# A two-layer convolution block on one core: the first convolution of images 3 to 7 in 64x32 tiles with a half-exchanged copy, and a new order of the work around it

## The chip, the cores and the metric

The kernel runs on one core of a Trainium2 chip. Its five engines run programs of their own and meet only at semaphores: TensorE (PE), VectorE (DVE), ScalarE (ACT), GpSimd (POOL), and SyncE (SP), which issues the DMAs. The metric is the device time of one execution in microseconds (us).

## The reference

Eight images of 32 channels, 128x128 pixels, float32. Cut to what is computed:

```python
x = x + conv0(quantised(_gn(x))) * (sx * sw / 127**2) + bias   # 3x3, int8 values, one scale sx over all eight images
h = lrelu(instnorm(disco_conv(_gn(x), weight1)))               # 3x3 kernel from a fixed basis
x = x + lrelu(instnorm(disco_conv(h, weight2)))
# _gn: GroupNorm over 2 channels; instnorm: per image and channel
```

The disco kernels are zero at the four corners of their 3x3 window, so convolutions 1 and 2 have five taps, convolution 0 has nine. The scale `sx` needs the largest value over all images, so no convolution starts before all images are read and normalised once. After that each image goes through three convolutions, and each of the later two needs statistics over a whole image of what came before it.

## The kernel before

An image is stored as four quadrants of pixels (even and odd rows and columns), each with 32 channels on 32 partitions, so 128 partitions by 64x64 numbers. A tap that shifts by one pixel is then a move to another quadrant, for half of the output with a shift of one place in a tile padded to 66x66. A **unit** is 16 of an image's 64 rows, 1024 columns, in two PSUM banks; an image has four. The tile `ring` has three slots of one unit each, which the three convolutions fill in the order `ORDER` (convolution 1 of image t, convolution 0 of image t+2, convolution 2 of image t). `wait_slot` holds a unit back until the unit three places before it has been taken out of its slot.

**TensorE.** Convolution 0 (`conv0_pair`, line 1023 in the profile) reads the float16 tile `qpad` with matmuls of 128 rows by 32 columns of the array. Four of them, for the four output quadrants, run side by side: a *round*. A bank takes four rounds (own, side, vert, corn), a unit 8, an image 32. Convolutions 1 and 2 (`half_taps`, lines 965 and 971) read float32 tiles with matmuls of 64 rows by 32 columns. Eight run side by side, four writing one bank (L965), four the other (L971), and each matmul shows as two records in the trace. Such a convolution of a unit is a `first_half` and a `second_half`, with the row halves exchanged between the banks; the second half waits until the first has ended (`crossed`). `conv` orders them first 0, first 1, second 0, first 2, second 1, first 3, second 2, second 3. A `gather` (L929) is a small 128x128 matmul that adds statistics across partitions.

**VectorE** goes through `period(t)`: statistics of each unit of convolutions 1 and 2 (`conv_stats`, L810) straight from `ring`; at an image's end `spread_conv` (L817, L819), on which the gather waits, and `group_moments` (L718), which reads the gather's result; `x1_unit` (L794), which adds convolution 0's unit to x and so empties its slot; `x1_stats` (L800) on the sum; `output` (L827), the last addition of the image before.

**ScalarE** takes units of convolutions 1 and 2 out of `ring` after their statistics (`take`, L381), which empties the slot, and normalises: `make_h` (L404) makes the input of convolution 2, `make_a` (L394) that of convolution 1 of the next image, `norm_out` (L413) the part that `output` adds.

**GpSimd** turns moments into scales and shifts (`norm_c`, `norm_x1`: L539 to L551) and quantises image t+3 in `period` t in four pieces of three operations each (`quantise`: L619, L622, L627). The third writes `qpad`, the first of an image not before convolution 0 has finished the image before.

**SyncE** loads the images, and stores each finished one in two pieces (the last in four), in order.

A *period* is the stretch from one image's convolution 1 to the next one's. The one in which TensorE works on images 3 (convolutions 1 and 2) and 5 (convolution 0) stands for all below.

## Time and profile before

| | us |
|---|---|
| median of 3 runs (387.83 to 388.05) | 387.9 |
| the profiled execution: its time | 387.43 |
| the profiled execution: its span | 385.6 |
| PE busy | 298.4 |
| DVE busy | 278.2 |
| ACT busy | 234.8 |
| POOL busy | 159.9 |

The span runs from the first instruction to the last; 1.8 us of the profiled execution's time lie around it. The first 76 us read and normalise the images; from there to 370 us TensorE hardly stops. In the profile a row "x4" of PE is a group of four matmuls that start together; the distance from one row's start to that of the next round is the pace, and the duration beside it includes the way through the array.

### The profile page before, as it was taken

Reading aid. Unit: us, or ns where it says so; the run is one execution under the profiler, and the core shown is the slowest. Engines: PE = TensorE matmul, PEld = TensorE weight load, DVE = VectorE, ACT = ScalarE, POOL = GpSimd, SP = SyncE. Lnnn points to the kernel's source line nnn. Section 1 sums busy time; section 2 is a strip of 40 time slices with the busy share of each in tenths; the row PEclk is TensorE's granted clock in tenths of the full one; section 3 lists DMA queues with packets and bytes.
Section 4 is the critical chain, followed back from the end, with each engine's and each line's share of the span. In section 5 each row is a group of like instructions: output and inputs, shape, how many; then the busy total and the mean of one; then the engine's idle time right before and its main releaser. Section 6 shows DMA issues by size and latency. Waiting matters only on the chain.

```text
span 385.6 us, 11585 instructions
## 1 busy us (share of the span) xinstructions
PE 298.4 (77%) x5224; PEld 121.5 (31%) x5224; DVE 278.2 (72%) x418; ACT 234.8 (61%) x243; POOL 159.9 (41%) x248
## 2 busy tenths in 40 slices
PE   0000100297999999999999999999999999999950
PEld 0000100253343334333433343333334343333320
DVE  3828899879969559857974995599559857544575
ACT  1079996295534674476528654754674478856554
POOL 0189886338949622932492067209621002100100
PEclk9999999999999999999999999999999999999985
DMA  7999600000000005001400220050005001400055
GB/s 272 398 426 428 267 1 1 0 2 2 3 2 2 3 2 220 3 2 59 164 3 3 115 106 3 3 219 4 2 2 221 2 2 58 165 3 2 2 219 218
DMA packets 4176, 34.77 MB, mean 90 GB/s; under 512 B 608, under 2 KB 768, under 8 KB 1280
## 3 DMA queue, kind: packets, MB, share of 16 engines
q1 hardware_dynamic: 4128, 34.04, 21.6%
q8 instruction: 41, 0.67, 0.7%
q14 instruction: 7, 0.06, 0.1%
HBM read 17.26 MB, written 16.78 MB: 88 GB/s over the span
## 4 chain that ended last, share of the span: by engine, by line
PE 60%; DVE 27%; POOL 5%; issue 3%; DMA 2%; ACT 1%; SPq 0%; DVEq 0%; POOLq 0%
PE ring L965 46%; PE ring L1023 8%; DVE amax L745 8%; DVE xs L827 7%; DVE bn_c L810 6%; PE ring L971 4%; DMA xs<-w_dram 2%; POOL apad L571 2%; DVE xs L794 2%; PE gathered_in L929 1%; DVE bn_x L800 1%; DVE bn_x L723 1%; ACT scaled L364 1%; POOL xs L510 1%; DVE qpad L787 1%
## 5 line engine op out<-in xcount | busy, mean ns | idle before, releaser
L810 DVE BATCH_NORM_STATS2 bn_c<-ring 128x6 f32<-128x512 f32 x128 | 82.7, 687 | 59.3 <-PE ring L971 59.3
L539 POOL TENSOR_SCALAR var_eps_c<-moments_c 128x1 f32<-128x1 f32 x16 | 3.1, 192 | 166.2 <-DVE moments_c L718 166.2
L971 PE MATMUL ring<-apad,own 64*32 64x512 f32 x448 | 58.7, 591 | 0.0
L965 PE MATMUL ring<-apad,own 64*32 64x512 f32 x448 | 58.6, 590 | 0.0
L971 PE MATMUL ring<-hpad,own 64*32 64x512 f32 x448 | 58.6, 591 | 0.0
L965 PE MATMUL ring<-hpad,own 64*32 64x512 f32 x448 | 58.6, 590 | 0.0
L971 PE MATMUL ring<-apad,side 64*32 64x512 f32 x448 | 58.4, 588 | 0.0
L965 PE MATMUL ring<-apad,vert 64*32 64x512 f32 x448 | 58.3, 587 | 0.0
L971 PE MATMUL ring<-hpad,side 64*32 64x512 f32 x448 | 58.3, 587 | 0.0
L965 PE MATMUL ring<-hpad,vert 64*32 64x512 f32 x448 | 58.2, 587 | 0.0
L381 ACT COPY apad<-ring 128x1024 f32<-128x1024 f32 x28 | 28.4, 1013 | 47.8 <-DVE bn_c L810 47.1
L381 ACT COPY hpad<-ring 128x1024 f32<-128x1024 f32 x28 | 28.4, 1014 | 27.8 <-DVE bn_c L810 27.3
L404 ACT ACTIVATE hpad<-hpad,shift_c,scale_c 128x1024 f32<-128x1024 f32 (+2 forms) x28 | 32.8, 1235 | 14.7 <-POOL shift_c L551 14.7
L413 ACT ACTIVATE apad<-apad,shift_c,scale_c 128x1024 f32<-128x1024 f32 x28 | 34.1, 1242 | 12.0 <-POOL shift_c L551 12.0
L794 DVE SCALAR_TENSOR_TENSOR xs<-ring,dequant,xs 128x1024 f32<-128x1024 f32 x32 | 39.9, 1274 | 1.9 <-PE ring L1023 1.9
L800 DVE BATCH_NORM_STATS2 bn_x<-xs 128x6 f32<-128x512 f32 x64 | 39.4, 678 | 0.0
L394 ACT ACTIVATE apad<-xs,shift_x,scale_x 128x1024 f32<-128x1024 f32 (+2 forms) x28 | 33.2, 1238 | 4.7 <-POOL shift_x L548 4.7
L827 DVE SCALAR_TENSOR_TENSOR xs<-apad,bias,xs 128x1024 f32<-128x1024 f32 x28 | 35.0, 1269 | 0.0
L745 DVE TENSOR_REDUCE amax<-apad 128x1 f32<-128x4096 f32 (+1 forms) x7 | 26.3, 3788 | 8.4 <-POOL apad L571 8.4
L619 POOL TENSOR_SCALAR scaled<-xs,q_scale,q_shift 128x1024 f32<-128x1024 f32 (+2 forms) x24 | 28.8, 1201 | 0.0
L331 ACT ACTIVATE qpad<-xs 128x4096 f16<-128x4096 f32 x5 | 18.0, 3608 | 16.9 <-DMA xs<-x_dram 16.9
L1042 PE MATMUL gathered_gn<-spread_x,const 128*128 128x24 f32 x6 | 1.8, 388 | 32.3 <-DVE spread_x L731 32.3
(139 smaller groups left out, 622.7 us busy)
## 6 DMA issues: line engine op xcount, KB each, us to landing
xs<-x_dram SPq DMA_DIRECT2D x8, 2048.0 KB, 10.1
out_dram<-xs SPq DMA_DIRECT2D x14, 1024.0 KB, 4.3
out_dram<-xs SPq DMA_DIRECT2D x4, 512.0 KB, 2.8
xs<-w_dram SPq DMA_DIRECT2D x1, 288.0 KB, 9.2
const<-const_dram SPq DMA_DIRECT2D x1, 146.0 KB, 2.4
xs<-w_dram SPq DMA_DIRECT2D x1, 36.0 KB, 1.7
bias<-bias_dram SPq DMA_DIRECT2D x1, 0.5 KB, 2.3
```

What stands on the lines that cost most here:

```text
L381: nc.scalar.copy(unit_of(tile, u), grid(slot(v, t, u))).then_inc(taken[v], 1)
L394: nc.scalar.activation(rows_of(a_tile(b), r0, r1), grid(xs_rows(b, r0, r1)), ACT.Identity, bias=param(shift["x1"], b), scale=param(scale[" ...
L404: nc.scalar.activation(rows, rows, ACT.Prelu, bias=param(shift["c1"], t), scale=param(scale["c1"], t), alpha=SLOPE).then_inc(h_ready, 1)
L413: nc.scalar.activation(rows, rows, ACT.Prelu, bias=param(shift["c2"], t), scale=param(scale["c2"], t), alpha=SLOPE).then_inc(out_norm, 1)
L745: nc.vector.tensor_reduce(amax[:, n:n + 1], gn_tile(b)[:, c0:c1], AX.X, ALU.max, apply_absolute_value=True).then_inc(max_done, 1)
L794: nc.vector.scalar_tensor_tensor(x, slot(0, b, u), dequant[:], x, ALU.mult, ALU.add).then_inc(taken[0], 1)
L800: ins = nc.vector.bn_stats(bn["x1"][:, k, :], xs_cols(b, k * BANK, BANK))
L810: ins = nc.vector.bn_stats(bn[s][:, u * UBANKS + h, :], ring_of(v, t, u)[:, h, :])
L827: nc.vector.scalar_tensor_tensor(x, unit_of(a_tile(t), u), bias[:], x, ALU.add, ALU.add).then_inc(out_ready, 1)
L965: nc.tensor.matmul(bank_out(t, u, v, hp, C * (2 * px + py), C), wv[q0:q0 + 64, v - 1, px, py, :], window(tile, u * UBANKS + hp, dy, 0, q0, ...
L971: ins = nc.tensor.matmul(bank_out(t, u, v, hx, C * (2 * px + py), C), ws[q0:q0 + 64, v - 1, px, py, :], window(tile, u * UBANKS + hx, 0, d ...
L1023: ins = nc.tensor.matmul(bank_out(b, u, 0, h, C * (2 * px + py), C), w[:, px, py, :], window(tile, u * UBANKS + h, dy, dx), start=part == ...
```

## The change

1. **Convolution 0 of images 3 to 7** is no longer done by `conv0_pair` but by `taps0`, in 64x32 tiles: six groups of four matmuls for a half unit, eight of them side by side, so 3 rounds for a half unit, 6 for a unit and 24 for an image. The nine taps fit because a second float16 tile `qturn` holds `qpad` with its two partition halves exchanged; the corner tap reads it in one of the two banks (`turn0` are its weights), where the other bank reads the side tap from `qpad`. `first0` waits for `qturn` (semaphore `q_turned`), `second0` for the end of its `first0` (`crossed0`).
2. **`turn(b)`** on SyncE fills `qturn` with two DMAs of 64 partitions once image b is quantised and convolution 0 of image b-1 is done. It stands in SP's queue between the stores of images.
3. **Order on TensorE** (`conv0_and_2`): the gather of convolution 1's statistics stands behind three half units; `first_half(2, t, 0)` stands in front of `second0(b, 3)`.
4. **Order on VectorE** in `period`, for all images: `group_moments("c1", t)` directly behind `spread_conv(1, t)`, the four `x1_unit`s together, two of the four `output`s of the image before behind them, and `x1_stats` mixed with the statistics of convolution 2.
5. **Room**: one tile `scaled` in place of two. It also holds `kern` and `kern0`, and small tiles share one. `quantise` therefore waits for each earlier piece, ScalarE's first quantising steps write to `hpad` without a wait for VectorE, GpSimd waits once for `weights12_ready`, and ScalarE makes four more small copies for `turn0`.

The diff, cut to its core:

```diff
@@ -96,7 +96,8 @@
         qpad = sb("qpad", [P, PAD, PAD], F16)
-        scaled = [sb(f"scaled{p}", [P, QCOLS], F32) for p in range(2)]
+        qturn = sb("qturn", [P, PAD, PAD], F16)
+        scaled = sb("scaled", [P, QCOLS], F32)
...
@@ -137,12 +133,13 @@
         var_eps_x = sb("var_eps_all", [P, B], F32)
-        kern = sb("kern", [P, 2 * TAPS * C], F32)[0:C].rearrange("p (v k o) -> p v k o", v=2, k=TAPS)
-        kern0 = sb("kern0", [P, TAPS * C], F16)[0:C].rearrange("p (k o) -> p k o", o=C)
-        centre = sb("centre", [P, 1], F32)
-        var_eps = {s: sb(f"var_eps_{s}", [P, 1], F32) for s in STAGES[1:]}
-        scale = {s: sb(f"scale_{s}", [P, 2], F32) for s in STAGES[1:]}
-        shift = {s: sb(f"shift_{s}", [P, 2], F32) for s in STAGES[1:]}
+        kern = scaled[0:C, 0:2 * TAPS * C].rearrange("p (v k o) -> p v k o", v=2, k=TAPS)
+        kern0 = scaled[0:C, 2 * TAPS * C:].bitcast(F16)[:, 0:TAPS * C].rearrange("p (k o) -> p k o", o=C)
+        var_eps_tile = sb("var_eps", [P, 3], F32)
+        var_eps = {s: var_eps_tile[:, n:n + 1] for n, s in enumerate(STAGES[1:])}
+        params = sb("params", [P, 2, 6], F32)
+        scale = {s: params[:, 0, 2 * n:2 * n + 2] for n, s in enumerate(STAGES[1:])}
+        shift = {s: params[:, 1, 2 * n:2 * n + 2] for n, s in enumerate(STAGES[1:])}
...
@@ -247,6 +246,9 @@
         gn_cut = COLS // 2
+        TURNED = 3
...
@@ -291,6 +293,17 @@
                 load(b)
+            def turn(b):
+                if b > TURNED:
+                    sp.wait_ge(conv_done[0], UNITS * b)
+                sp.wait_ge(q_ready, 4 * b)
+                for half in range(2):
+                    to, at = 64 * half, 64 * (1 - half)
+                    sp.dma_start(qturn[to:to + 64, 1:1 + BLK, :], qpad[at:at + 64, 1:1 + BLK, :]).then_inc(q_turned, 16)
+            turn(TURNED)
             for t in range(B):
...
@@ -298,12 +311,14 @@
                                  xs_cols(t, n * cols, cols)).then_inc(stored_first if t < 4 else stored, 16)
+                if t + 4 < B:
+                    turn(t + 4)
             sp.wait_ge(stored_first, 16 * 8)
             sp.wait_ge(stored, 16 * (2 * (B - 5) + 4))
         @block.scalar
         def _(act):
-            def assemble(kernel, own, side, vert, corn):
+            def assemble(kernel, own, side, vert, corn, turned):
...
@@ -317,7 +332,8 @@
                         if corn is not None:
-                            last = nc.scalar.copy(corn[q, 1 - qx, 1 - qy, :], k[:, 1 - dx, 1 - dy, :])
+                            nc.scalar.copy(corn[q, 1 - qx, 1 - qy, :], k[:, 1 - dx, 1 - dy, :])
+                            last = nc.scalar.copy(turned[q, qx, 1 - qy, :], k[:, 1 + dx, 1 - dy, :])
                 return last
...
@@ -359,15 +375,14 @@
                 r0, r1 = EDGES[n:n + 2]
-                if n >= 2:
-                    act.wait_ge(q_ready, n - 1)
-                nc.scalar.activation(scaled[n % 2][:, 0:(r1 - r0) * BLK], xs_rows(0, r0, r1), ACT.Identity,
+                nc.scalar.activation(flat(hpad)[:, r0 * BLK:r1 * BLK], xs_rows(0, r0, r1), ACT.Identity,
                                      bias=q_shift[:, 0:1], scale=q_scale[:, 0:1]).then_inc(q_scaled, 1)
             def affine_one(n):
                 r0, r1 = EDGES[n:n + 2]
+                act.wait_ge(q_ready, n + 1)
                 nc.scalar.activation(flat(hpad)[:, r0 * BLK:r1 * BLK], xs_rows(1, r0, r1), ACT.Identity,
...
@@ -613,9 +628,9 @@
                 r0, r1 = EDGES[n:n + 2]
-                rows = scaled[n % 2][:, 0:(r1 - r0) * BLK]
+                rows = scaled[:, 0:(r1 - r0) * BLK]
                 at = 4 * (b - 2) + n
-                pool.wait_ge(q_ready, 4 * (b - 1) + max(n - 1, 0))
+                pool.wait_ge(q_ready, 4 * (b - 1) + n)
                 nc.gpsimd.tensor_scalar(rows, xs_rows(b, r0, r1), q_scale[:, b:b + 1], q_shift[:, b:b + 1],
...
@@ -638,6 +653,7 @@
             norm_x1(0)
+            pool.wait_ge(weights12_ready, 1)
             quant_pieces(2, 0)
...
@@ -839,26 +856,24 @@
                     output(t - 1, 1)
-                    output(t - 1, 2)
                 conv_stats(1, t, 2)
-                if before:
-                    output(t - 1, 3)
                 conv_stats(1, t, 3)
                 spread_conv(1, t)
                 if t == 0:
                     group_moments("x1", 1)
-                x1_unit(t + 2, 0)
                 group_moments("c1", t)
-                x1_unit(t + 2, 1)
+                for u in range(UNITS):
+                    x1_unit(t + 2, u)
+                if before:
+                    output(t - 1, 2)
+                    output(t - 1, 3)
                 x1_stats(t + 2, 0)
-                x1_unit(t + 2, 2)
-                x1_unit(t + 2, 3)
+                conv_stats(2, t, 0)
                 x1_stats(t + 2, 1)
                 x1_stats(t + 2, 2)
+                conv_stats(2, t, 1)
                 x1_stats(t + 2, 3)
                 spread_stats("x1", t + 2)
-                conv_stats(2, t, 0)
-                conv_stats(2, t, 1)
                 conv_stats(2, t, 2)
...
@@ -993,10 +1008,11 @@
-            def conv(v, t, gathers=()):
-                first_half(v, t, 0)
+            def conv(v, t, gathers=(), begun=False):
+                if not begun:
+                    first_half(v, t, 0)
                 first_half(v, t, 1)
...
@@ -1027,6 +1043,53 @@
+            def taps0(b, u, hp, start, stop):
+                hx = 1 - hp
+                for n in range(3):
+                    for px in range(2):
+                        for py in range(2):
+                            q0, dy = 64 * px, 1 if py else -1
+                            tile, w, dy, dx = ((qpad, own0, 0, 0), (qpad, vert0, dy, 0),
+                                               (qturn, turn0, dy, 1 if px else -1))[n]
+                            nc.tensor.matmul(bank_out(b, u, 0, hp, C * (2 * px + py), C), w[q0:q0 + 64, px, py, :],
+                                             window(tile, u * UBANKS + hp, dy, dx, q0, 64),
+                                             start=start and n == 0, stop=stop and n == 2)
+                    for px in range(2):
+                        for py in range(2):
+                            q0, dx, dy = 64 * (1 - px), 1 if px else -1, 1 if py else -1
+                            w, dy, dx = ((own0, 0, 0), (vert0, dy, 0), (side0, 0, dx))[n]
+                            ins = nc.tensor.matmul(bank_out(b, u, 0, hx, C * (2 * px + py), C), w[q0:q0 + 64, px, py, :],
+                                                   window(qpad, u * UBANKS + hx, dy, dx, q0, 64),
+                                                   start=start and n == 0, stop=stop and n == 2)
+                return ins
+            def first0(b, u):
+                wait_slot(0, b, u)
+                pe.wait_ge(q_turned, 32 * (b - TURNED + 1))
+                taps0(b, u, 0, True, False).then_inc(crossed0, 1)
+            def second0(b, u):
+                pe.wait_ge(crossed0, UNITS * (b - TURNED) + u + 1)
+                taps0(b, u, 1, False, True).then_inc(conv_done[0], 1)
+            def conv0_and_2(b, t):
+                first0(b, 0)
+                first0(b, 1)
+                second0(b, 0)
+                gather("c1", t)
+                first0(b, 2)
+                second0(b, 1)
+                second0(b, 2)
+                first0(b, 3)
+                first_half(2, t, 0)
+                second0(b, 3)
+                conv(2, t, begun=True)
             counts = [0, 0]
...
@@ -1055,11 +1118,14 @@
                 conv(1, t, [("c2", t - 1), ("x1", t + 1)] if t >= 1 else ())
-                conv0_pair(t + 2, 0, gather_after=("x1", 1) if t == 0 else None)
-                conv0_pair(t + 2, 1, gather_after=("c1", t))
-                conv0_pair(t + 2, 2)
-                conv0_pair(t + 2, 3)
-                conv(2, t)
+                if t + 2 >= TURNED:
+                    conv0_and_2(t + 2, t)
+                else:
+                    conv0_pair(t + 2, 0, gather_after=("x1", 1))
+                    conv0_pair(t + 2, 1, gather_after=("c1", t))
+                    conv0_pair(t + 2, 2)
+                    conv0_pair(t + 2, 3)
+                    conv(2, t)
             conv(1, B - 2, [("c2", B - 3), ("x1", B - 1)])
```

VectorE in a period, from the statistics of convolution 1's third unit. In the rows of before, L810 are `conv_stats`, L827 `output`, L794 `x1_unit`, L800 `x1_stats`, L718 the moments:

```order
L810 BN_STATS bn_c<-ring 128x6 x2
L827 SCALAR_TENSOR_TENSOR xs<-apad,bias,xs 128x1024
L810 BN_STATS bn_c<-ring 128x6 x2
L817 BN_AGGR own_stat_c<-bn_c 128x2
L819 TENSOR_TENSOR spread_c<-const,own_stat_c 128x12
L794 SCALAR_TENSOR_TENSOR xs<-ring,dequant,xs 128x1024
L718 BN_AGGR moments_c<-gathered_in 128x2
L794 SCALAR_TENSOR_TENSOR xs<-ring,dequant,xs 128x1024
L800 BN_STATS bn_x<-xs 128x6 x2
L794 SCALAR_TENSOR_TENSOR xs<-ring,dequant,xs 128x1024 x2
L800 BN_STATS bn_x<-xs 128x6 x6
```

The same place in the changed kernel, where L827 are `conv_stats`, L844 `output`, L811 `x1_unit`, L817 `x1_stats`, L735 the moments:

```order
L827 BN_STATS bn_c<-ring 128x6 x4
L834 BN_AGGR own_stat_c<-bn_c 128x2
L836 TENSOR_TENSOR spread_c<-const,own_stat_c 128x12
L735 BN_AGGR moments_c<-gathered_in 128x2
L811 SCALAR_TENSOR_TENSOR xs<-ring,single,xs 128x1024 x4
L844 SCALAR_TENSOR_TENSOR xs<-apad,single,xs 128x1024 x2
L817 BN_STATS bn_x<-xs 128x6 x2
L827 BN_STATS bn_c<-ring 128x6 x2
L817 BN_STATS bn_x<-xs 128x6 x4
L827 BN_STATS bn_c<-ring 128x6 x2
L817 BN_STATS bn_x<-xs 128x6 x2
```

An output stood between the statistics of the third and the fourth unit, and another in front of the third; now two stand behind the fourth `x1_unit`, ahead of the statistics of convolution 2's first unit.

TensorE at the end of convolution 0, before: its last bank, then the first half of convolution 2's first unit (L965 and L971).

```order
L1023 MATMUL ring<-qpad,own 32x512 x4
L1023 MATMUL ring<-qpad,side 32x512 x4
L1023 MATMUL ring<-qpad,vert 32x512 x4
L1023 MATMUL ring<-qpad,corn 32x512 x4
L965 MATMUL ring<-hpad,own 32x512 x4
L971 MATMUL ring<-hpad,own 32x512 x4
L965 MATMUL ring<-hpad,vert 32x512 x4
L971 MATMUL ring<-hpad,side 32x512 x4
```

The same place now: the last rows of `first0(b, 3)` (L1057 and L1064 are `taps0`), the first half of convolution 2's first unit (L980 and L986), and `second0(b, 3)`.

```order
L1057 MATMUL ring<-qturn,turn 32x512 x4
L1064 MATMUL ring<-qpad,side 32x512 x4
L980 MATMUL ring<-hpad,own 32x512 x4
L986 MATMUL ring<-hpad,own 32x512 x4
L980 MATMUL ring<-hpad,vert 32x512 x4
L986 MATMUL ring<-hpad,side 32x512 x4
L1057 MATMUL ring<-qpad,own 32x512 x4
L1064 MATMUL ring<-qpad,own 32x512 x4
L1057 MATMUL ring<-qpad,vert 32x512 x4
L1064 MATMUL ring<-qpad,vert 32x512 x4
L1057 MATMUL ring<-qturn,turn 32x512 x4
L1064 MATMUL ring<-qpad,side 32x512 x4
```

Two groups of four make a round of eight here, and convolution 0's last half unit has moved behind four rows of convolution 2.

## Rows read from the trace of the kernel before

**Rows 1.** The page: busy time, and TensorE and its granted clock in 40 slices.

```profile
PE 298.4 (77%) x5224; PEld 121.5 (31%) x5224; DVE 278.2 (72%) x418; ACT 234.8 (61%) x243; POOL 159.9 (41%) x248
...
PE   0000100297999999999999999999999999999950
...
PEclk9999999999999999999999999999999999999985
```

**Rows 2.** Busy time by stretch (from:to, length, then each engine's): five periods; convolution 0 of one.

```profile
132.77:313.63 180.86, 180.20 (x3238) 70.20 (x3230) 135.27 (x210) 109.27 (x101) 69.49 (x106) 1.00 0.15 61
...
219.74:227.58 7.84, 7.70 (x146) 3.58 (x145) 7.60 (x11) 4.26 (x4) 3.26 (x5) 1.00 0.45 181
```

**Rows 3.** TensorE's timeline, end of convolution 1 to convolution 2: start, duration, what.

```profile
217.48 0.61 PE L971 MATMUL ring<-apad,side 64*32 64x512 f32 x4
...
218.74 0.61 PE L965 MATMUL ring<-apad,vert 64*32 64x512 f32 x4
...
219.17 0.61 PE L965 MATMUL ring<-apad,vert 64*32 64x512 f32 x4
219.20 0.61 PE L971 MATMUL ring<-apad,side 64*32 64x512 f32 x4
219.74 0.41 PE L1023 MATMUL ring<-qpad,own 128*32 128x512 f16 x4
...
222.17 0.39 PE L1023 MATMUL ring<-qpad,corn 128*32 128x512 f16 x4
222.69 0.39 PE L929 MATMUL gathered_in<-spread_c,const 128*128 128x12 f32 x2
223.01 0.41 PE L1023 MATMUL ring<-qpad,own 128*32 128x512 f16 x4
...
227.19 0.39 PE L1023 MATMUL ring<-qpad,corn 128*32 128x512 f16 x4
227.51 0.63 PE L965 MATMUL ring<-hpad,own 64*32 64x512 f32 x4
```

**Rows 4.** TensorE's timeline around that gather in the first period, image 0.

```profile
113.86 0.39 PE L1023 MATMUL ring<-qpad,corn 128*32 128x512 f16 x4
...
114.50 0.41 PE L1023 MATMUL ring<-qpad,own 128*32 128x512 f16 x4
```

**Rows 5.** VectorE's timeline: start, duration, what, [idle before <-releaser].

```profile
218.35 1.28 DVE L810 BATCH_NORM_STATS2 bn_c<-ring 128x6 f32<-128x512 f32 x2
219.56 1.26 DVE L827 SCALAR_TENSOR_TENSOR xs<-apad,bias,xs 128x1024 f32<-128x1024 f32 x1
220.75 1.28 DVE L810 BATCH_NORM_STATS2 bn_c<-ring 128x6 f32<-128x512 f32 x2
...
222.47 0.17 DVE L819 TENSOR_TENSOR spread_c<-const,own_stat_c 128x12 f32<-128x12 f32 x1
222.56 1.28 DVE L794 SCALAR_TENSOR_TENSOR xs<-ring,dequant,xs 128x1024 f32<-128x1024 f32 x1
223.75 0.20 DVE L718 BATCH_NORM_AGGREGATE moments_c<-gathered_in 128x2 f32<-128x12 f32 x1
224.13 1.28 DVE L794 SCALAR_TENSOR_TENSOR xs<-ring,dequant,xs 128x1024 f32<-128x1024 f32 x1 [0.17 <-PE ring L1023]
```

**Rows 6.** ScalarE's timeline: a take, the first pieces of convolution 2's input, the start.

```profile
219.67 1.01 ACT L381 COPY hpad<-ring 128x1024 f32<-128x1024 f32 x1 [1.43 <-DVE bn_c L810]
...
225.28 4.66 ACT L404 ACTIVATE hpad<-hpad,shift_c,scale_c 128x1088 f32<-128x1088 f32 x4 [2.20 <-POOL shift_c L551]
...
79.34 2.32 ACT L364 ACTIVATE scaled<-xs,q_shift,q_scale 128x1024 f32<-128x1024 f32 x2 [0.23 <-DVE qpad L787]
```

**Rows 7.** GpSimd's timeline: first and last write of the next image to qpad.

```profile
227.82 1.10 POOL L627 TENSOR_SCALAR qpad<-scaled 128x1088 f16<-128x1088 f32 x1 [0.16 <-POOL scaled L622]
...
238.12 1.00 POOL L627 TENSOR_SCALAR qpad<-scaled 128x960 f16<-128x960 f32 x1
```

**Rows 8.** DMA issues: count, KB each, us from issue to landing.

```profile
out_dram<-xs SPq DMA_DIRECT2D x14, 1024.0 KB, 4.3
```

34 lines of the change are left out of this document (16 added, 18 removed).

## The prediction

> **What bounds the kernel now.** I read the page first: PE is busy 77% of the span, but in the 40 slices it stands at 9 tenths from the tenth on and at the full granted clock, so in the middle nothing is to be had but by giving TensorE less to do or a wait less [rows 1]. Busy time by stretch says the same: of five periods, 180.86 us, PE is busy 180.20, DVE 135.27, ACT 109.27, POOL 69.49. A period is 36.17 us, of which convolution 0 takes 7.84 [rows 2]. Then TensorE's timeline: convolution 1's last round starts at 219.17, a round of eight float32 matmuls later than the one at 218.74, so 0.43 us is their pace; convolution 0 runs from 219.74 to 227.51 with the gather inside [rows 3]. The other engines' timelines say what they would be late with, if TensorE came sooner [rows 5, 6].
>
> **Convolution 0's rounds.** From 223.01 to 227.19 there are 19 rounds of four, 0.22 us each [rows 3]. 32 rounds are 7.04 us. The change makes 24 rounds of eight. If such a round also takes 0.22, as it streams the same 512 float16 columns, an image costs 5.28 and a half unit 0.66: **1.76 saved**. No float16 round of eight is in this trace. What the float32 ones show: the second four start 0.03 us after the first four (219.17 and 219.20) [rows 3], so the array takes eight tiles at nearly one time, and their 0.43 us per record is a pace of float32. That is the nearest row for the shape, and the float16 rounds the nearest for the data. I take 0.22; the upper bound is 0.43.
>
> **Changes of shape.** Between the last round of convolution 1 and the first of convolution 0 lie 219.74 - 219.17 = 0.57 us, not 0.43; on the way back 227.51 - 227.19 = 0.32, not 0.22 [rows 3]. All rounds are 64x32 now: **0.24 saved**. A change between float16 and float32 alone is in no row; below by nothing, above by these 0.24, I take nothing.
>
> **The gather.** It stretches 0.22 to 223.01 - 222.17 = 0.84 us [rows 3]. In the first period, where the statistics were ready, to 0.64 [rows 4]: so 0.20 is a wait for VectorE, whose statistics of the fourth unit start at 220.75 behind an output of 1.19 us [rows 5]. New: the fourth unit's last matmuls end at 219.20 + 0.61 = 219.81 [rows 3], and I take 0.1 us from there to VectorE. Statistics at 219.91; the spread ends 222.64 - 220.75 = 1.89 later [rows 5], at 221.80. The gather's turn comes at 221.90 (next part), so **0.20 saved**, and the gather costs some 0.44 with its changes of shape.
>
> **What is late next: four waits of TensorE.** Followed in the trace's own clock, from 219.60, where convolution 1's pace ends. Half units of float32 take 4 x 0.43 = 1.72. Spacing on VectorE is 1.21 for statistics (218.35 to 219.56) and 1.19 for output and x1_unit; a stage is complete some 1.28 after its start [rows 5]. A take costs 1.01, starting 0.04 behind its statistics [rows 6].
> - *Second unit of convolution 0.* Its slot is that of convolution 1's third unit, whose last matmuls end at 217.48 + 0.61 = 218.09 [rows 3]. Statistics 218.19 to 219.47, take to 220.53, TensorE at 220.58. It could start at 219.60 + 0.66 = 220.26, since `first0` of the first unit is only three rounds: **wait 0.32**. Before, this slot was wanted only at 221.5. Then 221.24, `second0` 221.90, gather 222.34, and the fourth take (221.24 to 222.26) is just in time.
> - *Convolution 2's first half.* Gather's matmul at 222.05, done 0.39 later [rows 3]; moments at 222.48. From moments to the first piece of `make_h` it is 225.28 - 223.75 = 1.53 [rows 5, 6], and 1.24 for the piece: 225.25, TensorE at 225.30. Four half units bring TensorE from 222.34 to 224.98: **wait 0.32**. The slot, that of the second x1_unit, is free at 225.15.
> - *Convolution 2's fourth unit.* `second0(b, 3)` now ends behind that half, at 225.30 + 1.72 + 0.66 = 227.68. The fourth x1_unit starts at 227.91, outputs take it to 231.48, x1 statistics to 232.69, and only then come the statistics of convolution 2's first unit (done at 233.97) and its take, 235.03. TensorE is through four half units at 227.68 + 6.88 = 234.56 and wants that slot: **wait 0.52**.
> - *Next convolution 1's second unit.* VectorE's queue stays full after that: five more statistics and 0.94 of spreading put the third unit's at about 239.8, its take at 242.1, where TensorE wants the slot at 235.08 + 3 x 1.72 + 1.72 = 241.96: **wait 0.1**.
>
> **Sum.** Per period -1.76 - 0.24 - 0.20 + 0.32 + 0.32 + 0.52 + 0.1 = -0.94. Five images, 3 to 7: -4.7. Check: convolution 2 then ends at 240.24 where it was 227.51 + 32 x 0.43 = 241.27, so -1.03 and 0.1 given back.
> At the start ScalarE's third piece no longer waits 0.23 for VectorE [rows 6], on the way to the first convolution: -0.2. The memsets, the four copies and the wait for `weights12_ready` lie where these engines idle: 0; if they did not, the four copies of 32 partitions would cost less than one take, 1.01, once. Outputs keep the stores' order; the last period's are as before: 0.
> *The copies.* GpSimd's first write to `qpad` now waits for `second0(b, 3)`, at 227.9 about when it stood before; its last write ended at 238.12 + 1.00 [rows 7], and each piece now waits some 0.15 for itself: 239.7. The two DMAs move 64 x 8448 bytes each, together about one 1024 KB store, 4.3 us to landing [rows 8]. `qturn` is there at about 245, needed at 219.60 + 35.2 = 254.8: hidden, with 10 us to spare. The store queued behind it is asked for only after 250.
> Total -4.9, less a tenth for the first of the five periods, which inherits nothing and gives nothing: **-4.8**. The profiled execution's own time is 387.43, so 382.6; it lies 0.47 below the median of 387.9, so the prediction is **383.1**.
>
> **Rivals.**
> 1. *The sum as above*, rounds 0.22 to 0.24: 57%. Each 0.01 on a round is 24 x 5 x 0.01 = 1.2 us less gained, but part of it hides in the waits. With the waits each 0.1 larger or smaller, 381 to 385.
> 2. *TensorE cannot feed rounds of eight float16 tiles.* Both shapes show one matmul record per 0.054 us (0.22 / 4 and 0.43 / 8) [rows 3]. If that is a limit of issue or of PSUM, a round takes 0.43, 24 of them 10.3, so +3.3 per image; less 0.44 for shapes and gather, +0.1 of waits left: +2.9, five times less 0.2 is +14, **402**. For it: the equal pace. Against: both paces equal the columns at the granted full clock. 10%.
>  The Trainium skill, "TensorE: Matmul & The Clock Gate", Part 1 ("Wait — 56ns, not 53.3ns?"), has two floors between starts: about 25 ns, and about 62 ns where microcode decodes matmuls. By the first, eight take 0.20 and nothing changes; by the second 192 matmuls take 11.9 us and the result is near 411. The 0.055 us per matmul seen here is under the second, so it isn't in force.
> 3. *Rounds between*, 0.26 to 0.30, issue falling a little short with eight weight loads a round: at 0.29 an image's rounds cost the 7.0 of before, shapes and gather give 0.44, the waits for VectorE take it back: **387** give or take 2. 10%.
> 4. *The waits don't appear* (takes or statistics come some tenths sooner): 5 x 2.2 + 0.2 = 11.2, **376.7**; half of it is more likely than all. 8%.
> 5. *Slower through VectorE*: the fourth x1_unit is held behind half of convolution 2, and behind it VectorE has thirteen stages without a gap. Each tenth more on this chain is a tenth more per period, at convolution 2's fourth unit or at the next period's start. It decides once it is 0.94 us later than I work out, which takes up the whole gain; at 1.3 us later the result is 5 x 0.36 = 1.8 above no gain, less the 0.2 of the start: **389.5**. For it: VectorE's spare time, 9.1 us a period [rows 2], lies in other places. Against: each stage is a row of fixed length. 12%.
> 6. *The copy comes late*: only beyond 14 us for 1 MB; at 20 us it would cost 5 x 5, **408**. Against: 4.3 us for a like store. 3%.
>
> **Numbers.** Likeliest 383.1, its own range 381 to 385.5. For 8 in 10 the range takes in rival 3, rival 5 and the near half of rival 4: 379 to 389.5. A measurement of this kernel tells about 0.2%, 0.8 us, from no change. Faster: 57, 8, half of 3 and a third of 5, 74%. Same: 6%. Slower: 20%.
>
> **What would show it.** Rows of `taps0` 0.22 us apart (rivals 2 and 3 else). No gap of shape between the convolutions. PE idle before the second unit of convolution 0 for ScalarE's take, 0.3 us; before L980 on `hpad` for `make_h`, 0.3; in convolution 2's fourth unit for a take, 0.5; VectorE without idle time from the fourth x1_unit to convolution 2's last statistics; a period of 35.2 us. The `qturn` DMAs landing 10 us before use. I would be wrong above all if the pace of eight is not that of four, or if the chain on VectorE is longer.

## The result, and the profile after

The changed kernel takes **382.87 us** (median of 4 runs, 382.57 to 383.94) against 387.98 (387.83 to 388.4) for the kernel before on the same chip: ratio 0.9865, 95% interval 0.984 to 0.989. The profiled execution took 382.87 us, its span is 381.1 us. The forecast was 383.1, and 382.6 for a profiled execution like the one of before.

First the page: busy time, and two rows of the 40 slices.

```profile
PE 291.4 (76%) x5544; PEld 119.8 (31%) x5544; DVE 278.6 (73%) x421; ACT 234.9 (62%) x247; POOL 168.3 (44%) x248
...
PE   0000100197999999999999999999999999999950
...
PEclk9999999999999999999999999999999999999995
```

TensorE has 7.0 us less to do than in [rows 1], and still stands at 9 tenths throughout. The stretch of five periods shows the other side: a stretch 4.2 us shorter than five periods of before holds 3.5 us without a matmul, where [rows 2] has 0.7. The line gives the stretch, its length, then what PE, PEld, DVE, ACT and POOL were busy in it, the granted clock, and the DMA share and GB/s.

```profile
136.20:312.84 176.64, 173.18 (x3559) 69.14 (x3551) 134.92 (x210) 108.69 (x100) 78.06 (x106) 1.00 0.27 88
```

A gather stands inside each convolution 1 (that of convolution 2 of the image before); where it starts is the mark of a period. Here are two marks in TensorE's timeline, after and then before (the second fence):

```profile
206.86 0.39 PE L944 MATMUL gathered_in<-spread_c,const 128*128 128x12 f32 x2
...
242.20 0.39 PE L944 MATMUL gathered_in<-spread_c,const 128*128 128x12 f32 x2
```

```profile
208.71 0.39 PE L929 MATMUL gathered_in<-spread_c,const 128*128 128x12 f32 x2
...
244.89 0.39 PE L929 MATMUL gathered_in<-spread_c,const 128*128 128x12 f32 x2
```

35.34 us against 36.18. The five periods of either kernel agree within 0.02 us, so this mark tells 0.02 us where whole executions differ by 1 to 3 us; the experiments are read by it. Of the 4.56 us between the spans (381.08 against 385.64) 0.17 lies ahead of the first mark (136.20 against 136.37), 4.24 in the periods (the last mark is at 312.84 against 317.25), 0.15 behind them.

TensorE's timeline of the same place as [rows 3]: the end of convolution 1, convolution 0 (L1057 and L1064 are `taps0`), convolution 2 (L980, L986), and its fourth unit.

```profile
217.32 0.61 PE L980 MATMUL ring<-apad,vert 64*32 64x512 f32 x4
...
217.75 0.41 PE L1057 MATMUL ring<-qpad,own 64*32 64x512 f16 x4
217.77 0.42 PE L1064 MATMUL ring<-qpad,own 64*32 64x512 f16 x4
...
218.19 0.40 PE L1057 MATMUL ring<-qturn,turn 64*32 64x512 f16 x4
...
218.74 0.40 PE L1057 MATMUL ring<-qpad,own 64*32 64x512 f16 x4
...
219.85 0.38 PE L1057 MATMUL ring<-qturn,turn 64*32 64x512 f16 x3
...
220.19 0.39 PE L944 MATMUL gathered_in<-spread_c,const 128*128 128x12 f32 x2
220.51 0.40 PE L1057 MATMUL ring<-qpad,own 64*32 64x512 f16 x4
...
222.94 0.38 PE L1057 MATMUL ring<-qturn,turn 64*32 64x512 f16 x3
...
223.59 0.63 PE L980 MATMUL ring<-hpad,own 64*32 64x512 f32 x4 [0.25 <-ACT hpad L419]
...
232.41 0.64 PE L980 MATMUL ring<-hpad,vert 64*32 64x512 f32 x4
...
233.42 0.63 PE L980 MATMUL ring<-hpad,own 64*32 64x512 f32 x4 [0.34 <-ACT apad L396]
```

To see: from the round at 220.51 to the one at 222.94 there are 11 steps of 0.22 us, with eight matmuls in a round. No gap of shape stands at 217.32 to 217.75 (0.43, the pace). Three gaps are new: 218.19 to 218.74, 222.94 to 223.59, 232.41 to 233.42. The bracket gives only the part of a wait in which nothing ran in the array (0.25, 0.34); the wait is the distance of the starts less the pace: 0.33, 0.43 and 0.58.

VectorE's timeline behind convolution 1, as [rows 5], and the two ScalarE rows on which those gaps hang:

```profile
220.62 0.21 DVE L735 BATCH_NORM_AGGREGATE moments_c<-gathered_in 128x2 f32<-128x12 f32 x1 [0.64 <-PE gathered_in L944]
220.75 3.83 DVE L811 SCALAR_TENSOR_TENSOR xs<-ring,single,xs 128x1024 f32<-128x1024 f32 x3
226.25 1.28 DVE L811 SCALAR_TENSOR_TENSOR xs<-ring,single,xs 128x1024 f32<-128x1024 f32 x1 [1.68 <-PE ring L1064]
227.45 2.47 DVE L844 SCALAR_TENSOR_TENSOR xs<-apad,single,xs 128x1024 f32<-128x1024 f32 x2
229.84 1.28 DVE L817 BATCH_NORM_STATS2 bn_x<-xs 128x6 f32<-128x512 f32 x2
231.04 1.28 DVE L827 BATCH_NORM_STATS2 bn_c<-ring 128x6 f32<-128x512 f32 x2
```

```profile
222.15 4.64 ACT L419 ACTIVATE hpad<-hpad,params 128x1088 f32<-128x1088 f32 x4 [1.74 <-POOL params L566]
232.35 1.02 ACT L396 COPY apad<-ring 128x1024 f32<-128x1024 f32 x1 [5.56 <-DVE bn_c L827]
```

VectorE idles 1.68 us for the half unit that now ends behind half a unit of convolution 2, then works without a pause; the first statistics of convolution 2 start at 231.04, the take at 232.35 ends at 233.37, and TensorE's fourth unit starts 0.05 later.

### The profile page after: what moved, and what is told of

Same layout as the page of the kernel before. It is cut to its first block, busy times and chain, and to the rows that moved or that the text cites. A ratio compares the mean times of both kernels' runs of the same rounds, so it can differ in the third digit from the quotient of the medians.

```text
span 381.1 us, 12247 instructions
## 1 busy us (share of the span) xinstructions
PE 291.4 (76%) x5544; PEld 119.8 (31%) x5544; DVE 278.6 (73%) x421; ACT 234.9 (62%) x247; POOL 168.3 (44%) x248
## 4 chain that ended last, share of the span: by engine, by line
PE 54%; DVE 27%; ACT 6%; POOL 6%; issue 3%; DMA 3%; SPq 0%; DVEq 0%; POOLq 0%
PE ring L980 43%; DVE amax L762 8%; DVE xs L844 5%; DVE bn_c L827 4%; PE ring L986 3%; DVE xs L811 3%; DVE bn_x L817 3%; PE ring L1057 3%; DMA xs<-w_dram 3%; PE ring L1039 2%; POOL apad L586 2%; ACT hpad L419 2%; PE gathered_in L944 1%; ACT apad L396 1%; ACT hpad L396 1%
## 5 line engine op out<-in xcount | busy, mean ns | idle before, releaser
L827 DVE BATCH_NORM_STATS2 bn_c<-ring 128x6 f32<-128x512 f32 x128 | 82.1, 687 | 43.4 <-PE ring L986 43.4
L554 POOL TENSOR_SCALAR var_eps<-moments_c 128x1 f32<-128x1 f32 x16 | 3.0, 190 | 145.0 <-DVE moments_c L735 145.0
L980 PE MATMUL ring<-hpad,own 64*32 64x512 f32 x448 | 59.2, 591 | 2.9 <-ACT apad L396 1.7
L980 PE MATMUL ring<-hpad,vert 64*32 64x512 f32 x448 | 58.9, 587 | 0.0
L986 PE MATMUL ring<-hpad,own 64*32 64x512 f32 x448 | 58.6, 592 | 0.0
L986 PE MATMUL ring<-apad,own 64*32 64x512 f32 x448 | 58.6, 591 | 0.0
L980 PE MATMUL ring<-apad,own 64*32 64x512 f32 x448 | 58.5, 591 | 0.0
L986 PE MATMUL ring<-apad,side 64*32 64x512 f32 x448 | 58.2, 587 | 0.0
L986 PE MATMUL ring<-hpad,side 64*32 64x512 f32 x448 | 58.1, 587 | 0.0
L980 PE MATMUL ring<-apad,vert 64*32 64x512 f32 x448 | 58.1, 587 | 0.0
L811 DVE SCALAR_TENSOR_TENSOR xs<-ring,single,xs 128x1024 f32<-128x1024 f32 x32 | 39.7, 1268 | 9.7 <-PE ring L1064 8.4
L419 ACT ACTIVATE hpad<-hpad,params 128x1024 f32<-128x1024 f32 (+2 forms) x28 | 32.7, 1234 | 12.3 <-POOL params L566 12.3
L817 DVE BATCH_NORM_STATS2 bn_x<-xs 128x6 f32<-128x512 f32 x64 | 39.8, 677 | 0.0
L428 ACT ACTIVATE apad<-apad,params 128x1024 f32<-128x1024 f32 x28 | 34.0, 1241 | 8.0 <-POOL params L566 8.0
L634 POOL TENSOR_SCALAR scaled<-xs,q_scale,q_shift 128x1024 f32<-128x1024 f32 (+2 forms) x24 | 37.4, 1556 | 1.8
L409 ACT ACTIVATE apad<-xs,params 128x1024 f32<-128x1024 f32 (+2 forms) x28 | 33.2, 1239 | 4.7 <-POOL params L563 4.7
L844 DVE SCALAR_TENSOR_TENSOR xs<-apad,single,xs 128x1024 f32<-128x1024 f32 x28 | 35.1, 1273 | 0.0
L642 POOL TENSOR_SCALAR qpad<-scaled 128x1024 f16<-128x1024 f32 (+2 forms) x24 | 25.2, 1048 | 8.9 <-PE ring L1064 7.1
```

The source lines that it names most:

```text
L409: nc.scalar.activation(rows_of(a_tile(b), r0, r1), grid(xs_rows(b, r0, r1)), ACT.Identity, bias=param(shift["x1"], b), scale=param(scale[" ...
L419: nc.scalar.activation(rows, rows, ACT.Prelu, bias=param(shift["c1"], t), scale=param(scale["c1"], t), alpha=SLOPE).then_inc(h_ready, 1)
L428: nc.scalar.activation(rows, rows, ACT.Prelu, bias=param(shift["c2"], t), scale=param(scale["c2"], t), alpha=SLOPE).then_inc(out_norm, 1)
L634: nc.gpsimd.tensor_scalar(rows, xs_rows(b, r0, r1), q_scale[:, b:b + 1], q_shift[:, b:b + 1], ALU.mult, ALU.add).then_inc(q_step_pool, 1)
L811: nc.vector.scalar_tensor_tensor(x, slot(0, b, u), dequant[:], x, ALU.mult, ALU.add).then_inc(taken[0], 1)
L817: ins = nc.vector.bn_stats(bn["x1"][:, k, :], xs_cols(b, k * BANK, BANK))
```

## The experiments

In the texts recorded ahead of the runs "the first convolution" is `conv1`, "the second" `conv2`, and "the third" `conv0`, the one with the new tiles; "the moments" are `group_moments("c1", t)`. Periods are the distance of the marks above in the profiled execution; the five of a kernel agree within 0.04 us where nothing else is said (the last is up to 0.4 shorter in some), and ratios are against the kernel before, run on the same chip. A "run" with a number is the experiment of that number. Medians of different kernels are compared with care: in some of the executions the granted clock falls for a while near the start, whatever the kernel, which costs about 1.5 us (last section), and the share of these executions differs from row to row. The period is free of that.

| kernel | median us | ratio, 95% interval | period us |
|---|---|---|---|
| before | 387.98 | | 36.17 |
| changed | 382.87 | 0.9865 (0.984 to 0.989) | 35.33 |
| 1: VectorE's order alone | 388.49 | 1.0008 (0.9988 to 1.0029) | 36.15 |
| 2: changed, VectorE's old order | 395.58 | 1.017 (1.013 to 1.021) | 37.81 |
| 3: changed, nothing in front of the last half (two runs) | 380.05, 380.03 | 0.9785 (0.974 to 0.983), 0.9797 (0.976 to 0.983) | 34.66, 34.64 |
| 4: both undone, tiles alone | 389.53 | 1.0018 (0.9991 to 1.0044) | 36.37 |
| 5: half of it in front | 379.77 | 0.9788 (0.976 to 0.981) | 34.76 |
| 8: nothing in front, last unit begun sooner | 379.02 | 0.9771 (0.975 to 0.980) | 34.66 |
| 7: nothing in front, first unit finished first | 379.02 | 0.9770 (0.974 to 0.980) | 34.56 |
| 8: both of these | 380.19 | 0.9790 (0.976 to 0.982) | 34.56 |
| 6: full tiles, 24 rounds | 378.78 | 0.9759 (0.973 to 0.979) | 34.27 |
| 9: each copy twice | 392.96 | 1.0125 (1.009 to 1.016) | 35.34 to 40.14 |
| 9: half of each copy again | 383.69 | 0.9879 (0.984 to 0.992) | 35.33, one 35.64 |

**1. VectorE's order alone.** The kernel before with the changed `period` of VectorE:

```diff
-                    output(t - 1, 2)
                 conv_stats(1, t, 2)
-                if before:
-                    output(t - 1, 3)
 ...
+                for u in range(UNITS):
+                    x1_unit(t + 2, u)
+                if before:
+                    output(t - 1, 2)
+                    output(t - 1, 3)
```

> The kernel before with one edit: VectorE's list of a period in the changed order (output pieces 2 and 3 behind the four x1 units, the statistics of the second convolution set between those of x1), while TensorE keeps the old full tiles, the old order of units and no turned copy. Theory A (the gain is the rounds saved by the 64-row tiles, the new order of VectorE only makes room for them): little by itself, 385.5 to 387.5 us, since the gather of the middle statistics no longer waits (0.20 us a period) and the fourth unit of the second convolution finds its bank later. Rival B (the order on VectorE is what pays, since the x1 units free the banks sooner): 383 to 384 us, as the changed kernel. Rival C (the order is a loss by itself, paid for by the tiles): 389 us or more.

388.49 us, no difference. The gather's 0.20 us did go (from gather to gather 13.78 us against 13.98), and 0.17 came back further on, a wait of 0.16 in the next convolution 1 among it. By itself the order gains nothing and costs nothing: rivals B and C fall, and theory A was 1 us too hopeful.

**2. The changed kernel with VectorE's old order.** The whole of VectorE's `period` as before, all else changed.

> The changed kernel with VectorE's list of a period as before (output pieces 1, 2 and 3 between the statistics of the first convolution, x1 statistics between the x1 units). Theory A with the chain of VectorE as a second bound (outputs ahead of the x1 units hold the banks of the units that TensorE now reaches 1.8 us sooner, and the third convolution's last unit comes behind half a unit of the second): slower than the changed kernel by 8 to 12 us, 391 to 395 us, above the kernel before. Rival R (the saved rounds carry the gain whatever VectorE does): 379 to 384 us.

395.58 us, 7.1 above the kernel before on that chip, and 0.6 above theory A's range; rival R falls. TensorE's rows of the same period:

```profile
230.99 0.63 PE L982 MATMUL ring<-hpad,own 64*32 64x512 f32 x4 [0.75 <-ACT hpad L419]
...
242.02 0.63 PE L982 MATMUL ring<-hpad,own 64*32 64x512 f32 x4 [1.53 <-ACT apad L396]
```

The same two gaps as in the changed kernel, 0.93 and 1.78 us in place of 0.43 and 0.58. The wait for the second unit's bank is 0.48 and not 0.33, and the gather costs 0.62 more. Together that is 2.47 of the 2.48 us by which the period grew, and more than the eight rounds saved. So the order is worth 12.4 us (5 x (37.81 - 35.33)) once the tiles are in, though it is worth nothing without them.

**3. Nothing in front of the last half.**

```diff
-                first_half(2, t, 0)
                 second0(b, 3)
-                conv(2, t, begun=True)
+                conv(2, t)
```

> The changed kernel with the second half of the third convolution's last unit issued ahead of the second convolution's first half (not behind it). Theory A (that half unit of 1.72 us ahead of the last unit delays the last x1 unit, which shows an idle gap of 1.68 us on VectorE, and everything that VectorE does behind it): faster than the changed kernel by 2 to 4.5 us, 378.5 to 381 us, with the gap on VectorE gone. Rival S (the half unit in front covers the wait for the bank and for the first h piece, so that its removal puts idle time on TensorE): slower than the changed kernel by 1 to 3 us, 384 to 386 us. Both as large as each other: 382.5 to 383.3 us.

380.05 us; and once more on the chip that ran the full tiles, the first unit finished first and the doubled copy:

> The kernel of the run without the half unit in front once more, on the chip of the next three, to compare them with. Theory A: 379 to 381 us, ratio 0.979 as before. If the 3 us between it and the changed kernel came from the starts of the runs (which differ by 1 to 2 us) it comes out at 382 us or more.

380.03 us. The period falls by 0.67 in the first run and by 0.69 in the second, whose timelines of VectorE and of TensorE are these:

```profile
219.24 5.02 DVE L811 SCALAR_TENSOR_TENSOR xs<-ring,single,xs 128x1024 f32<-128x1024 f32 x4
```

```profile
221.44 0.39 PE L1057 MATMUL ring<-qturn,turn 64*32 64x512 f16 x4
221.93 0.40 PE L1057 MATMUL ring<-qpad,own 64*32 64x512 f16 x4
...
222.39 0.39 PE L1057 MATMUL ring<-qturn,turn 64*32 64x512 f16 x4
222.61 0.60 PE L980 MATMUL ring<-hpad,own 64*32 64x512 f32 x4
```

The four `x1_unit`s run in one piece, the gap of 1.68 is gone, and with it both waits of convolution 2 (0.43 and 0.58). What the half unit in front did cover shows at 221.44 to 221.93: 0.27 us, in which `second0` waits for its own `first0` to leave the array. 0.43 + 0.58 - 0.27 = 0.74, of which the period shows 0.69; a wait of 0.03 in the next convolution 1 is part of the rest. At 222.39 to 222.61 float16 goes over to float32 at the pace of 0.22: the change of type alone costs nothing. Theory A holds and rival S falls: two of the forecast's four waits hang on this one line.

**4. Tiles alone.** Edits 2 and 3 together.

> Tiles and turned copy alone: the changed kernel with VectorE's list as before and with the last unit of the third convolution finished ahead of the second convolution. Theory A (VectorE's list binds as soon as TensorE is faster): about the time of the kernel before, 386 to 391 us, so that all of the rounds saved (some 9 us) go into waits for VectorE. Rival R (the rounds carry the gain): 379 to 382 us.

389.53 us, as the kernel before; theory A holds and rival R falls. Rounds and shapes saved 2.0 us a period, and waits of 0.48 (bank), 0.44 (the gather, beyond that of before), 0.27 (halves of the last unit) and 0.98 (fourth unit of convolution 2) took 2.2 back. Runs 2 to 4 and the changed kernel make a table of two by two: VectorE's order is worth 2.48 us a period with the half unit in front (37.81 against 35.33) and 1.72 without it (36.37 against 34.65); the half unit in front costs 1.44 with the old order and 0.68 with the new one. Each of the two losses is larger where the other stands.

**5. Half of it in front.**

```diff
-                first_half(2, t, 0)
+                wait_slot(2, t, 0)
+                pe.wait_ge(h_ready, 4 * t + 1)
+                half_taps(2, t, 0, h_tile(t), 0, False, True, False)
                 second0(b, 3)
+                half_taps(2, t, 0, h_tile(t), 0, True, False, False).then_inc(crossed, 1)
```

> The changed kernel with half of the half unit in front: two of the second convolution's four rounds (0.86 us) ahead of the third convolution's last half, two behind it. Theory A (the harm grows with the time that stands ahead of the last half): about midway between 380.0 us (nothing in front) and 382.9 us (1.72 us in front), 381 to 382 us. Rival D (what stands in front pays for itself once it covers the wait of 0.27 us between the two halves of the last unit, and 0.86 us is soon enough for VectorE): at or below the kernel with nothing in front, 378.5 to 380 us.

379.77 us, period 34.76: not midway between 34.65 and 35.33, but 0.11 above the first (run 3). Theory A's straight line was wrong. The time lies in rival D's range, and 0.86 us is soon enough for VectorE, as D has it; but what stands in front does not quite pay for itself. TensorE's and VectorE's rows:

```profile
221.28 0.38 PE L1057 MATMUL ring<-qturn,turn 64*32 64x512 f16 x1
221.92 0.63 PE L980 MATMUL ring<-hpad,own 64*32 64x512 f32 x4 [0.25 <-ACT hpad L419]
```

```profile
223.72 1.28 DVE L811 SCALAR_TENSOR_TENSOR xs<-ring,single,xs 128x1024 f32<-128x1024 f32 x1 [0.82 <-PE ring L1064]
```

The wait for the first h piece (the first part of convolution 2's input from `make_h`) is there in full, 0.43, more than the 0.27 that is covered; the one for the take in the fourth unit is gone, since VectorE's chain begins 0.86 us sooner and was late by 0.58 only. A wait of this sort is a difference between two chains: it shrinks with what one of them gains and then stays at zero.

**6. Full tiles, as many rounds.** Edit 1, in which `conv0_pair` of images 3 to 7 leaves out the part `corn`, so that the output lacks the corner taps: `parts = 3 if b >= 3 else 4`.

> No 64-row tiles and no turned copy: the kernel before with VectorE's new order, in which images 3 to 7 leave out the corner taps of the third convolution (24 rounds of full tiles a period, not 32), so its output leaves out these taps. It prices the 64-row tiles against full tiles of as many rounds. Theory A (a round of eight 64-row tiles costs what one of four full tiles does, 0.22 us, and what the shape adds is only that no change of shape stands between the convolutions, 0.24 us a period): 0.5 to 1.5 us slower than the kernel without the half unit in front, 380.5 to 382 us. Rival R (the 64-row tiles cost something hidden, in the copy or in the feed of TensorE): faster than it by 1 us or more, 379 us or less.

378.78 us, period 34.27, 0.37 less than with nothing in front: theory A had the sign wrong. The time is that of rival R, but not for R's reason, as TensorE's rows show. They are:

```profile
217.22 0.61 PE L963 MATMUL ring<-apad,vert 64*32 64x512 f32 x3
...
217.82 0.41 PE L1022 MATMUL ring<-qpad,own 128*32 128x512 f16 x4
...
223.37 0.39 PE L1022 MATMUL ring<-qpad,vert 128*32 128x512 f16 x4
223.69 0.63 PE L963 MATMUL ring<-hpad,own 64*32 64x512 f32 x4
```

The changes of shape are back (0.17 and 0.10) and no other gap stands between, for one unit is finished before the next begins and needs no wait between halves. The 64-row tiles pay 0.33 (the second unit's bank) and 0.27 (between halves): 0.60 - 0.27 = 0.33 of the 0.37. The rounds themselves cost the same. (The rest, 0.04, I can't place.)

**7. The first unit finished first.**

```diff
                 first0(b, 0)
-                first0(b, 1)
                 second0(b, 0)
+                first0(b, 1)
```

and on VectorE `x1_unit(t + 2, 0)` ahead of `group_moments("c1", t)`.

> The kernel without the half unit in front, in which the third convolution's first unit is finished before its second is begun, and VectorE adds the first x1 unit ahead of the moments of the first convolution. It removes the wait of 0.33 us a period of the second unit for its bank. Theory A (VectorE's list is full from the first x1 unit on, so the wait moves to a later unit): within 0.7 us of the kernel without the half unit. Rival W (each wait seen on TensorE is worth its length): 1.5 to 2 us faster than that kernel, 378.5 us or less. Rival M (the moments behind an x1 unit hold back ScalarE's h pieces by 1.2 us): 2 to 6 us slower.

379.02 us, period 34.56, 0.08 less. The wait of 0.33 for the bank is gone, and one of 0.27 between `first0` and `second0` stands in its place. Theory A's result, by the periods (5 x 0.08 = 0.4 us; the medians differ by 1.0, but by 0.3 among the executions with a mean granted clock of 0.984 and more, 378.97 against 379.30), with another cause: it was TensorE's own halves, not VectorE's list, that took it. Rivals W and M fall.

**8. The last unit's first half sooner** (`first0(b, 3)` ahead of `second0(b, 2)`), on the kernel of run 3 (kernel 3) and on that of run 7 (kernel 7).

> The kernel without the half unit in front, in which the first half of the last unit of the third convolution stands ahead of the second half of the unit before it, so that the wait of 0.27 us between the halves of the last unit is covered. Theory W (this wait is worth its length, since TensorE is the bound of these kernels): 378.4 to 379.3 us, period 34.4 us against 34.64. Theory V (the second half of the third unit comes 0.65 us later, and VectorE's x1 units with it): 0 to 1.6 us slower, 380 to 381.7 us.

> Both edits of TensorE's order: the first unit finished before the second is begun (with the first x1 unit ahead of the moments), and the last unit's first half ahead of the third unit's second half. With nothing in front there was a period of 34.56 us for the first edit alone. Theory W (each wait of TensorE that is taken away is worth its length): period 34.3 us, 377.7 to 378.6 us, the lowest of all with the full computation. Theory V (VectorE gives it back): 379 to 380.5 us.

379.02 and 380.19 us. Both medians stay within the spread of their bases, and the periods don't move at all: 34.66 and 34.56. On kernel 3 the wait of 0.27 between the halves is gone, and TensorE's timeline shows what took its place:

```profile
219.84 0.39 PE L1057 MATMUL ring<-qturn,turn 64*32 64x512 f16 x4
220.25 0.40 PE L1057 MATMUL ring<-qpad,own 64*32 64x512 f16 x4
...
230.42 0.59 PE L980 MATMUL ring<-hpad,vert 64*32 64x512 f32 x1
230.98 0.63 PE L980 MATMUL ring<-hpad,own 64*32 64x512 f32 x4
```

0.19 at the bank of the last unit, 0.14 at the take for convolution 2's fourth unit. On kernel 7 the 0.27 goes whole into the wait for the first h piece (TensorE starts at 223.30, 0.14 behind that piece's end). Theory W's median for kernel 3 (378.4 to 379.3) came in, its period (34.4) did not, and the period is the finer measure; on kernel 7 both missed. VectorE gives it back, as theory V has it, but the price is nothing and not up to 1.6 us. In this order of units TensorE gains nothing by its own waits: statistics, takes and h pieces come no sooner.

**9. Each copy twice, and half of it again.** SP makes both DMAs, waits until they have landed, and makes both again, or one of them (`range(3)`, 48 for 64):

```diff
-                for half in range(2):
-                    to, at = 64 * half, 64 * (1 - half)
+                for half in range(4):
+                    to, at = 64 * (half % 2), 64 * (1 - half % 2)
+                    if half == 2:
+                        sp.wait_ge(q_turned, 64 * (b - TURNED) + 32)
```

> The changed kernel, in which each half-exchanged copy is made twice, one pass behind the other, before TensorE may read it. One pass took 6.2 us in the median (4.4 to 7.2) and landed at 247.4 us in the profiled period, 5.7 us ahead of its first reader at 253.1 us. Theory A (the copy is hidden, with about 6 us to spare): two passes are late by 0 to 1.5 us a period, so 382.9 to 390 us, with TensorE's wait in front of the first round of the third convolution and nowhere else. The prediction's 10 us to spare: 382.5 to 383.5 us, no wait. Rival K (the copy is on the path now): 35 us more, 6 to 7 us a period.

> The changed kernel, in which one of the two halves of each turned copy is copied once more behind the first pass. Two whole passes in a row took 14.7 us where 12.9 were to be had. With one pass of 7.2 us and then a lone half of about 4.4 us the copy lands some 11.6 us after its issue, 1.3 us ahead of its first reader. Theory A (nothing is paid until the copy lands behind the last matmul ahead of its reader): 382.5 to 383.5 us, no wait. Rival T (the copy's traffic slows other work in proportion to its length): 385 us or more, with no wait at the reader.

Twice: 392.96 us, above theory A's range and far below rival K's. The row of the list of waits (us in all, times, longest):

```profile
PE ring L1059 <- DMA qturn<-qpad: 9.0, 4, 3.4
```

9.0 us in four periods, more than the 1.5 a period allowed for; the four are 1.5 to 4.8 us longer. Two things were missed: two passes kept the reader waiting until 15.4 us after their issue (168.81 to 184.22), and the waits of 2.24 and 3.39 us were each followed by a lower clock (below). Half again: 383.69, 0.2 above theory A's range; four periods as in the changed kernel and one longer by 0.3, with a wait of 0.41 for the copy. In those four the second pass made the copy 4.2 to 5.0 us longer, in that one 5.8. So theory A's mechanism holds, and rival T falls: the copy costs nothing as it is, nor up to 5.0 us longer, and begins to at 5.8.

## Why the prediction was right

Term by term, per period, forecast and then measured:

| step of the forecast | forecast | measured |
|---|---|---|
| 24 rounds of eight for 32 of four | -1.76 | -1.74 (24 x 0.221 = 5.30) |
| no change of shape | -0.24 | -0.24 |
| the gather's wait | -0.20 | -0.18 (219.85 to 220.51 is 0.66, was 0.84) |
| second unit of convolution 0, for a take | +0.32 | +0.33 |
| convolution 2's first half, for `make_h` | +0.32 | +0.43 |
| convolution 2's fourth unit, for a take | +0.52 | +0.58 |
| next convolution 1's second unit | +0.1 | 0 |
| sum | -0.94 | -0.82 (the marks: -0.84) |

- *The rounds.* Rival 2 (TensorE can't feed eight float16 tiles) and rival 3 (0.26 to 0.30) fall by the rows from 220.51 to 222.94. A record each 0.028 us is well under the 0.054 that both shapes of before had in common.
- *The waits.* Each was worked out by following one chain from row to row, and the three that came stand where they were put. The one for `make_h` was mis-sized by 0.11: the moments came 0.43 behind the gather and the piece 1.53 behind them, as forecast, but from the piece's start to TensorE's it is 1.44 us (222.15 to 223.59), not 1.29; TensorE's own side took back 0.04. The piece takes 1.30 us, in the trace of before too (225.28 to 226.58), where the prediction has 1.24, and TensorE follows 0.14 behind its end, not 0.05. The fourth unit's came out 0.06 larger, nearly all of it because the fourth x1_unit starts 0.28 behind the end of TensorE's last round at 225.97, and not 0.23. The last wait doesn't appear. Rival 4 (none appear) and rival 5 (the chain longer by 0.94 and more) fall with these; how near rival 5 was shows run 2, where VectorE's old order, with outputs and x1 statistics between the same stages, costs 12.4 us.
- *The start*: -0.2 forecast, the first mark is 0.17 earlier. The starts of the kernels traced differ by up to 2.7 us (first marks from 135.53 to 138.24), so this is no proof.
- *The copy*: hidden, as forecast, but the step "together about one 1024 KB store, 4.3 us" is wrong, and so is "10 us to spare". SP's row, and the copy's own DMA row:

```profile
240.21 1.11 SPq L304 DMA_DIRECT2D qturn<-qpad  x2
```

```profile
DMA to landing us min/median/max: 4.4/6.2/7.2
```

Of this period's two the later one, issued at 240.72, took 6.9 us and landed at 247.6, 5.5 us ahead of its reader at 253.09 (the text ahead of run 9 took the longest landing for it, and has 247.4 and 5.7). 2 us more of the room went to GpSimd (last section). The rates are in the windows with the copy, and with a store:

```profile
241.50:246.00 4.50, 4.50 (x84) 1.77 (x76) 1.67 (x4) 3.13 (x3) 2.20 (x7) 1.00 0.93 212
252.20:254.00 1.80, 1.77 (x48) 0.62 (x32) 1.38 (x3) 0.99 (x1) 0.00 (x0) 1.00 1.06 437
```

The DMA engines are busy in both (share 0.93 and 1.06), but move 212 GB/s in the copy and 437 in the store. The later of the two landed 2.1 us behind the earlier one, which was issued 0.5 us ahead of it (245.5 and 247.6). The Trainium skill, "SBUF — State Buffer", section "Can I just issue two DMAs to hit both halves?", says that two DMAs, one on partitions from 0 and one on partitions from 64, run one after the other, and that only one transfer over all 128 partitions reaches all ports. By that rule, the trace agrees: about half of the rate. It was the rule to use for the copy's price.
- *The sum over the kernel.* 4.24 of the periods, 0.17 of the start and 0.15 of the end make 4.56 where 4.8 was forecast (the tenth that the first period was to gain less is not seen: 35.33, as the others). The medians differ by 5.1. That the median came within 0.2 us of the forecast is in part luck, since it also hangs on how far each kernel's profiled execution lies from its median: 0.47 for the kernel before when the prediction was made, 0 for the changed one.

What the forecast did not ask is whether the waits had to be. It took the half unit in front of `second0(b, 3)` for given and priced what it delays; runs 3 and 5 show that this one line costs 0.6 to 0.7 us a period, near as much as the whole change gains. Without it the kernel takes 379 to 380 us, below both kernels.

## What to carry to other kernels

When an engine at 9 tenths gets less to do, its rows tell exactly what is saved; what is left of it is decided by the buffers that it now wants sooner. Follow each buffer from the last write through statistics and copy to the next write, and subtract: waits of 0.3 to 0.6 us came out within 0.11 here. Order and saved work are no sum: here VectorE's order was worth nothing alone and 12.4 us with the tiles (8.6 with nothing in front of the last half), and the tiles nothing without it. Work put in front of the end of a stage covers a small wait on its own engine (0.27 us) and delays all that hangs on that end (by 1.72 us); compare the two, and put in front no more than the next engine has to spare. Where executions differ by 1 to 3 us, the distance between marks in the steady part settles tenths.
